# Transposing x1 on VectorE in 32x32 blocks instead of on TensorE, with the token sums taken from DRAM

## The reference

```python
x = x + _layernorm(attn(_layernorm(x)))       # attn: qkv, softmax(q k.T / 16) v, Wo, bo
x = x + _layernorm(ffn(_layernorm(x)))        # ffn: (silu(xt @ W_gate.T) * (xt @ W_up.T)) @ W_down.T, F = 2752
```

## Time and profile before

| | us |
|---|---|
| median of 3 runs | 1672.58 (1672.29 to 1673.23) |
| profiled execution | 1671.54 |
| its span in the trace | 1669.4 |
| granted TensorE clock, share of full | 0.999 |
| TensorE busy | 1651.3 (99% of the span) |
| VectorE busy | 1112.2 (67%) |
| ScalarE busy | 637.5 (38%) |
| GpSimd busy | 481.7 (29%) |
| DMA, mean over the span | 190 GB/s |

### The profile page before, as it was taken

The page is one execution under the profiler, slowest core; times in us unless marked ns, Lnnn a source line. Parts: engine busy times, 40 slices in busy tenths (PEclk is TensorE's granted clock), DMA queues, the critical chain, the costliest instruction groups (busy, mean ns, idle before and its releaser), DMA issues.

```text
span 1669.4 us, 20939 instructions
## 1 busy us (share of the span) xinstructions
PE 1651.3 (99%) x7672; PEld 1372.9 (82%) x7672; DVE 1112.2 (67%) x1625; ACT 637.5 (38%) x1149; POOL 481.7 (29%) x409
## 2 busy tenths in 40 slices
PE   7999999999999999999999999999999999999998
PEld 6888888888888888888888888888888888888887
DVE  7875677777866666666557777855655555654676
ACT  3323344445533332333246544322323333344551
POOL 3230554554345445454111102411211111200003
PEclk9999999999999999999999999999999999999999
DMA  7542564567464546464578766844444554487772
GB/s 293 202 176 78 196 219 154 176 214 254 168 221 145 170 146 191 158 216 159 171 251 320 232 205 191 261 142 139 139 142 142 160 163 147 140 284 249 226 257 101
DMA packets 161716, 317.13 MB, mean 190 GB/s; under 512 B 13008, under 2 KB 41808, under 8 KB 158672
## 3 DMA queue, kind: packets, MB, share of 16 engines
q1 hardware_dynamic: 161616, 315.82, 56.7%
HBM read 212.21 MB, written 103.56 MB: 189 GB/s over the span
## 4 chain that ended last, share of the span: by engine, by line
PE 93%; DVE 4%; DMA 1%; issue 1%; ACT 0%; POOL 0%; SPq 0%; DVEq 0%; POOLq 0%; ACTq 0%
PE ps L343 28%; PE ps L345 28%; PE ps L344 28%; PE ps L1952 4%; PE ps L1848 3%; PE ps L1953 2%; PE ps L1897 1%; PE ps L1898 1%; DMA w_raw<-hsp_dram 1%; DVE y_all L1768 1%; DVE norm_x_stats L1301 0%; DVE xn_t L1320 0%; DMA x_tile<-x 0%; DVE slots L1320 0%; DVE y_all L1824 0%
## 5 line engine op out<-in xcount | busy, mean ns | idle before, releaser
L1320 DVE TENSOR_TENSOR slots<-w_raw,slots 128x512 fp32r<-128x512 f32 x500 | 406.9, 835 | 267.4 <-ACT slots L1125 267.2
L1125 ACT CAST slots<-w_raw 128x512 fp32r<-128x512 f32 x504 | 302.1, 621 | 471.4 <-PE ps L345 461.1
L343 PE MATMUL ps<-xc,slots 128*128 128x512 f32 x1208 | 470.9, 390 | 0.3 <-issue 0.3
L345 PE MATMUL ps<-xc,slots 128*128 128x512 f32 x1208 | 470.1, 389 | 0.0
L344 PE MATMUL ps<-xc,slots 128*128 128x512 f32 x1208 | 470.0, 389 | 0.0
L343 PEld LDWEIGHTS ps<-xc,slots 128*128 128x128 f32 x1208 | 226.7, 188 | 47.6 <-issue 0.7
L345 PEld LDWEIGHTS ps<-xc,slots 128*128 128x128 f32 x1208 | 226.7, 188 | 47.1
L344 PEld LDWEIGHTS ps<-xc,slots 128*128 128x128 f32 x1208 | 226.8, 188 | 46.9
L343 PE MATMUL ps<-slots 128*128 128x512 f32 x572 | 222.6, 389 | 0.4 <-DVE slots L1320 0.4
L345 PE MATMUL ps<-slots 128*128 128x512 f32 x572 | 222.5, 389 | 0.0
L344 PE MATMUL ps<-slots 128*128 128x512 f32 x572 | 222.5, 389 | 0.0
(11 more groups left out here) (189 smaller groups left out, 2385.5 us busy)
## 6 DMA issues: line engine op xcount, KB each, us to landing
w_raw<-hsp_dram SPq DMA_DIRECT2D x154, 256.0 KB, 4.0
hsp_dram<-hs SPq DMA_DIRECT2D x20, 1792.0 KB, 8.3
w_raw<-wffn SPq DMA_DIRECT2D x134, 256.0 KB, 3.7
w_raw<-wffn SPq DMA_DIRECT2D x58, 512.0 KB, 6.2
w_raw<-wdt_dram SPq DMA_DIRECT2D x88, 256.0 KB, 3.7
wgt_dram<-tt SPq DMA_DIRECT2D x21, 1024.0 KB, 8.3
w_raw<-wgt_dram SPq DMA_DIRECT2D x84, 256.0 KB, 2.9
xc_raw<-xq_dram SPq DMA_DIRECT2D x9, 1024.0 KB, 6.7
```

Source lines behind the costliest of these rows:

```text
L343: pe.matmul(dst, stat(HIGH), mov(HIGH), start=first, stop=False, skip_group_check=reread)
L345: return pe.matmul(dst, stat(LOW), mov(HIGH), start=False, stop=last, skip_group_check=reread)
L1125: act.copy(operand(n, HIGH), source(n)).then_inc(w_high, 1)
L1320: return dve.tensor_tensor(dst, src, high.bitcast(F32), ALU.subtract)
```

## The change

VectorE transposes x1n in one instruction per tile, in 32x32 blocks, into x_cols, a buffer for four tiles (a block); nothing is transposed on TensorE for these tiles, and ScalarE's copies of them are gone. Since a block transposition leaves the 128 tokens of a tile in four groups of 32, the columns in xq_dram stand in "block order": column 128 a + 32 u + j is token 128 u + 32 a + j of the block (u the tile of the block, a the group of 32). SyncE stores a whole block at once in eight transfers of 256 KB from 32 partitions each (store_cols, in tiles 6, 10 and 14). The order within the last block is as it was. The token sums need both blocks in the same order, so they take all four parts from DRAM (load_first, 4 x 256 KB) into first_a1 and first_a2, work in place, and are done in tiles 11 to 14 (SUMS). The sums of weights move to tiles 9 and 10 (WGT = 8). load_res and store_out of blocks 0 to 2 read and write DRAM in column order (column_rows).

```diff
+SQ = 32
+WGT = KP + 1 - EARLY
+SUMS = 2 * TPB + 3
...
-    xt_tile = [at("xt_even", 188, [KC, P]), at("xt_odd", 148, [KC, P])]
-    xp_tile = at("xp_tile", 176, [2, KH, P])
-    s_tile = at("s_tile", 180, [4, KH, P])
+    x_cols = at("x_cols", 176, [KC, P // SQ, TPB, SQ])
+    first_a1 = at("first_a1", 148, [2, KH, P])
+    first_a2 = at("first_a2", 200, [2, KH, P])
...
+            def store_cols(b):
+                sp.wait_ge(cols_ready, TPB * b + TPB)
+                if b > 0:
+                    sp.wait_ge(xq_stored, 128 * b)
+                for g in range(2):
+                    for a in range(P // SQ):
+                        sp.dma_start(xq_dram[b // 2, b % 2, g, :, :, cols(a)].rearrange(
+                                         "(b j) k n -> j k b n", j=SQ),
+                                     x_cols[a * SQ:(a + 1) * SQ, KH * g:KH * g + KH, :, :, :].rearrange(
+                                         "j k b u i -> j k b (u i)")).then_inc(xq_stored, 16)
...
-            def load_partner(i):
-                sp.wait_ge(xs_done, 4 * i)
-                sp.wait_ge(xq_stored, 32 * (i + 1))
-                for g in range(2):
-                    sp.dma_start(xp_tile[:, g, :, :], xq_dram[0, 0, g, :, :, cols(i)]).then_inc(xp_loaded, 16)
+            def load_first(i):
+                sp.wait_ge(xq_stored, 256)
+                if i > 0:
+                    sp.wait_ge(xs_stored, 64 * i)
+                for block, tile in enumerate((first_a1, first_a2)):
+                    for g in range(2):
+                        sp.dma_start(tile[:, g, :, :], xq_dram[0, block, g, :, :, cols(i)]).then_inc(xp_loaded, 16)
...
+                if SUMS <= t < SUMS + TPB:
+                    load_first(t - SUMS)
                 if t == TILES - 1:
...
+                if t >= 6 and t % TPB == 2:
+                    store_cols(t // TPB - 1)
+                if SUMS <= t < SUMS + TPB:
+                    store_first_sums(t - SUMS)
                 store_x1(t - 2)
...
+            def column_rows(dram, block, i):
+                rows = dram[block * BLOCK:(block + 1) * BLOCK, :]
+                if block == BLOCKS - 1:
+                    return rows[i * P:(i + 1) * P, :]
+                return rows.rearrange("(u a j) c -> a u j c", u=TPB, j=SQ)[i]
...
             def load_res(P_, T, i, place):
-                sp.dma_start(res[:, place, :], x1_dram[row_block(2 * P_ + T, i), :]).then_inc(res_loaded[place], 16)
+                sp.dma_start(res[:, place, :], column_rows(x1_dram, 2 * P_ + T, i)).then_inc(res_loaded[place], 16)
...
+                pool.wait_ge(xp_loaded, 64 * i + 64)
+                pool.tensor_tensor(a22, a21, a22, ALU.add).then_inc(xs_done, 1)
...
                 if t == TILES - 1:
                     act.wait_ge(xs_stored, 64 * TPB)
-                    act.wait_ge(xq_stored, 32 * (LNT - 1))
+                    act.wait_ge(xq_stored, 32 * LNT)
...
+            def x1_blocks(u):
+                dve.wait_ge(x1n_done, u + 1)
+                if u >= TPB and u % TPB == 0:
+                    dve.wait_ge(xq_stored, 32 * u)
+                dve.transpose(x_cols[:, :, :, u % TPB, :].rearrange("p k b i -> p (k b) i"),
+                              x1n[:, u % 2, :].rearrange("p (m i) -> p m i", i=SQ)).then_inc(cols_ready, 1)
...
                     a_moments(t - 2)
+                if 3 <= t < last:
+                    x1_blocks(t - 3)
                 o_out(t - 1)
...
-                if t >= 4:
-                    transpose_x1n(t - 4, 0)
...
-                    if t >= 4 and g == 2:
-                        transpose_x1n(t - 4, 1)
```

More of the change, by code:

```diff
@@ L530, in store_rest_sum, with store_late @@
                 sp.dma_start(wrt_dram[:, :], w_raw[:, Q12, :]).then_inc(wgt_stored, 16)
-            def store_xq(u, g, tile):
-                sp.wait_ge(xq_evicted, 2 * u + g + 1)
-                if g == 0 and u > 0:
-                    sp.wait_ge(xq_stored, 32 * u)
-                b = u // TPB
-                sp.dma_start(xq_dram[b // 2, b % 2, g, :, :, cols(u % TPB)], tile).then_inc(xq_stored, 16)
+            def store_cols(b):
[8 more added lines that the diff above has]
+                                         "j k b u i -> j k b (u i)")).then_inc(xq_stored, 16)
+            def store_late(i, g, tile):
+                sp.wait_ge(xq_evicted, 2 * i + g + 1)
+                if g == 0:
+                    sp.wait_ge(xq_stored, 32 * (LNT + i))
+                sp.dma_start(xq_dram[1, 1, g, :, :, cols(i)], tile).then_inc(xq_stored, 16)
             def load_xc(P_, slot, block, g):
@@ L574, in _ @@
                     store_wdt(k)
[L575 removed]
+                if t == WGT:
                     load_rest()
                     load_pair(1, pair_buffer(0))
[L578 removed]
+                if t == WGT + 1:
                     store_sums(1)
                     load_pair(0)
[L581 to L589 removed]
                 if t == TILES - 1:
@@ L601, in _ @@
                     load_residual(t)
-                if t == KP + 3:
+                if t == WGT + 2:
                     store_sums(0)
@@ L680, in _ @@
                     for g in range(2):
-                        store_xq(LNT + i, g, res[:, 1, cols(g, BLOCK)].rearrange("p (k t) -> p k t", k=KH))
+                        store_late(i, g, res[:, 1, cols(g, BLOCK)].rearrange("p (k t) -> p k t", k=KH))
                 i = late_tile(p, LATE_LOAD)
@@ L1956, in weigh @@
                     last.then_inc(pv_ready, 1)
-            def transpose_x1n(u, g):
-                if g == 0:
-                    pe.wait_ge(x1n_done, u + 1)
-                else:
-                    pe.wait_ge(xq_evicted, 2 * u + 1)
-                transposes(7, KH * g, x1n[:, u % 2, :], KH).then_inc(xq_ready, 1)
             def attend(t):
```

77 lines of the change are left out of this document (23 added, 54 removed).

## The result

The changed kernel takes 1759.74 us (median of 6 runs, 1757.8 to 1761.04) against 1672.65 before; the ratio is 1.0521, 95% interval 1.0508 to 1.0535. It is 87 us slower where 34 were forecast, and lies outside the range. The span of the profiled execution is 1759.3 us against 1669.4, 89.9 more. Two much slower executions further on, 1837.64 us of rows16 and 5914.59 of early_out_plain, are not in the ratios.

What follows compares the result with a forecast made beforehand. TensorE, busy 99% of the span, was taken as the bound. Attention terms -5.4 + 8.4 + 3.8 + 2.6 = +9.4 and feed-forward +25 gave +34.4, 1707 us forecast, range 1677 to 1728.

Steps and rivals of the forecast that it cites:

- TensorE's saving: Tiles 4 to 14: without the transposes of x1n each falls from 16.84 to 16.35 us, -5.4 us together.
- VectorE's transposition: Each of twelve, between norm_a_moments and o_sum, takes 1.1 us, fits VectorE's idle gap and costs nothing.
- The loop of tiles 12 to 14: Sums, normalisation, x1 add, store and next loads take about 17.6 us against TensorE's 16.35: +3.8 us (1.2 to 6).
- Which transfers would go slowly and at what rate: Feed-forward part: 24 load_res and store_out transfers with outermost count 4 use four DMA engines, 99 GB/s, 5.3 us each.
- the start of the second pass: Eight stores and four loads on four engines, operand loads among them, outlast the operand buffers: +15 us (5 to 30).
- the end: The last four stores in groups overlap the kernel's end and cost nothing.
- Each group of four res loads: At about 925 and 1502 us: the operand load behind lands 11.6 us later, +5 each (0 to 11), together +10.
- Tile 15: ScalarE waits for column and sum stores before splitting A11, so o_half comes at 18.1 us: +2.6 (0 to 10).
- Tile 11's stall: Token sums wait for the block's return from DRAM, so VectorE normalises late and TensorE waits: +8.4 us (5.2 to 15.8).
- Sixteen engines: Rival: all sixteen DMA engines serve the 24 feed-forward transfers; +9.4, 1682 us (1675 to 1690); chance 0.18.
- Hidden stalls: Rival: the stalls are hidden and only TensorE's saving is left; 1667 us, faster; chance 0.08.
- VectorE as the bound: Rival: transposition takes 1.7 us or more and VectorE bounds tiles 4 to 14; +5.4 more, 1712 us; chance 0.06.

Runs made afterwards that it cites:

- rows16: Kernel before, with load_res and store_out of blocks 0 to 2 in 16 groups of 8 rows, 32 rows apart: 1674.22 us.
- early_out_plain: plain_rows with sums a tile later, two buffer pairs for their loads, reordered tile 15, and last o_half ahead of ScalarE's wait for the sums' stores: 1671.34 us.
- rows4: Kernel before, with load_res and store_out of blocks 0 to 2 in 4 groups of 32 rows, 128 rows apart: 1740.01 us.
- plain_rows: Changed kernel, but load_res and store_out of blocks 0 to 2 take 128 rows in a row again: 1689.85 us.
- rows4_loads: rows4 with only the twelve load_res in 4 groups, the twelve store_out as before the change: 1708.28 us.
- a11_first: plain_rows with A11 loaded ahead of block 2's column stores and split before the weight operands, ScalarE's wait for the sums' stores behind the tile: 1682.94 us.
- split_rows: Changed kernel, row order correct, each of the 24 load_res and store_out transfers cut into four of 32 rows and 32 partitions: 1692.19 us.
- rows8: Kernel before, with load_res and store_out of blocks 0 to 2 in 8 groups of 16 rows, 64 rows apart: 1695.76 us.

## Why the prediction was wrong

**Right.** TensorE's saving: 16.35 us for a tile, measured 16.32 to 16.38 in tiles 4 to 11. That the first group of transposes is worth nothing: tile 9 keeps its 0.2 us of idle. VectorE's transposition: 1.1 us forecast, 1.19 measured, with 1.03 of gap left. The loop of tiles 12 to 14: 17.6 forecast, 17.9 and 18.0 measured. Which transfers would go slowly and at what rate: 99 GB/s forecast, 98 measured, with 4.1 packets of them under way at a time; rows4 and plain_rows show the form alone to be the cause.

**What failed.** The largest miss is at the start of the second pass, where the wait was the wrong one: operands were to be late, and a store was. Three other terms had the right wait and too small a size, the end was put at nothing and so was the lower clock. All six missed on the same side.

1. *Each group of four res loads, 5 us forecast, 17.5 and 16.5 measured (rows4_loads: 16.7 and 15.3).* The operand behind them was to land at 948.5, which in the shifted time of the changed kernel is 967.9; it landed 4.5 later, at 972.4. That was an error of working, and not of the price: the operand of before came at 936.95, and four loads of 5.3 us in place of 1.3 are 16.1 more and not 11.6. From 936.95 that makes 953.0, which is 972.4 in shifted time. TensorE's reserve I had as 9.5 us from where ScalarE begins to wait; ScalarE began at 953.84 and TensorE stood from 961.35, 7.5 after it. When the operand has come, the first conversion by ScalarE and VectorE comes before the first matmul, which cost 2.1 us (972.47 to 974.53) that the reserve hid before. And TensorE starts at the lower clock. Together that is 13.2 us of wait and 4.3 beside it.

2. *The start of the second pass, +15 forecast, +31.5 measured.* I reckoned with operands behind the transfers. What comes last is the store itself: ScalarE's copy of m1 writes where y_all was and waits for the fourth store (line 1210), 26.15 us where the row of before had 3.22. I named the row and took no price from it. Up to the fourth store four stores and two loads are issued, 6 x 5.3 = 32 us on four engines from 1039.33 on, with operands among them, so it lands after 1071 at the earliest, and ScalarE wants it at 1055.5 (1058.72 less 3.22): a wait of some 16 us or more could be worked out from rows 13 and 14. rows4_loads shows it: with the stores as they were 5.5 us are left of 32.2. TensorE stands twice, 17.2 and 11.3 us, and the rest is 3.0 us, the lower clock and smaller waits.

3. *Tile 15, +2.6 forecast, +9.1 with the third round of the loop (of which 1.3 was forecast).* I worked out when A11 lands by rates alone. Block 2's eight stores held SyncE for 8.48 us and the sums' for 4.02, so A11 was issued 13.6 us after the first of them, and it took 7.8 to land, not 2.6 + 2.0, behind all that stood in the queue. a11_first takes that away and the 6.6 us with it. And tile 15's stall is paid again after it, since TensorE ran the next stretch (424 to 428) at a granted clock of 0.50: 14.1 us for work of 11.5 (a11_first).

4. *Tile 11's stall, +8.4 forecast, VectorE 11.9 late.* The loads were to have landed 18.1 us into tile 11 and GpSimd could start at 22.0. The column stores ran at 222 GB/s, not 283: 9.4 us for 2.10 MB in place of 7.4, which is 2.0 of these 3.9. I had priced slow stores only in the high end (+7.4) and taken the rate of 128 partitions for the sum. The Trainium skill, "SBUF — State Buffer", section on the DMA port swizzle, has 189 GB/s measured for partitions 0 to 31. The runs have more than that (222 here, and 235 in split_rows with operands between), but its direction was right. The other 1.9 us lie between the issue of the loads and GpSimd's start, 10.1 us, and aren't separated further.

5. *The end, nothing forecast, +5.0 measured.* The last stores in groups were to overlap the end. rows4 has the same +5.0 there and rows4_loads none, so it is the stores'. The stores of the last block stand in the queue behind them: SyncE issues the sixth of all stores of that stage 3.6 us after the fifth (1741.38 and 1745.01), where it was 0.7 before.

**What no term held: the lower clock.** After each of the long waits TensorE does its first 2.8 to 4.6 us of work at a granted clock of 0.50. The five waits are 66.1 us (10.39, 13.18, 17.23, 11.26 and 14.03); the stages in which they lie are 77.4 us longer (11.95 over 16.35 for tile 12, 17.5, 31.5 and 16.5). In all TensorE is busy for 24.4 us of the trace at 0.50, 18.9 of them behind these five waits. Work at half the clock takes twice as long (a group of four transposes 1.12 us at 349.78, where it takes 0.60), so by estimate 9.5 of the 11.3 us between are the lower clock, and the rest small waits.

**The rivals.** Sixteen engines: out, by the row with share 0.26. Hidden stalls: out. VectorE as the bound: out, by the 1.19 us of the transposition. The range was too narrow because I set the high end by one term at its end, with the others at their middle, while three of them shared one cause (loads and stores on four engines hold up everything behind them in the queue) and missed on the same side.

The Trainium skill, "DMA: Bandwidth & Descriptors", section "Why a DMA increments its semaphore by 16 and not by 1", gives the number of engines as the largest up to 16 that divides the slowest dimension of both sides. The trace agrees: 4.1, 8.1 and 16.3 packets of the loads are under way at a time in rows4, rows8 and rows16. The time of the transfers doesn't follow from it alone, 26.0, 21.1 and 10.9 us, because a packet takes 159, 300 and 246 ns.

## What to carry to other kernels

An index change that costs nothing on the engines can change the form of every transfer that meets the new order: look at the outermost count of each, and at who waits for the transfer itself, not only for what is queued behind it. Twice the engines need not halve the time: 8 groups gained 5 us of 26 on 4. Where a queue has to swallow a block at once, work out the wait of the last reader from the issue times as well as from the bytes, and give it a tile of cover and a second buffer before taking work off the busiest engine. A stall of TensorE costs more than its length here, 1.5 to 4.3 us more for 10 to 17 us, so a sum of stalls has to carry that for each piece.

## What was not expected of the hardware

- Four loads of 512 KB in rows of 4 KB, 512 packets: 9.0 us with 128 rows in a row, 26.0 in 4 strided groups, 21.1 in 8 and 10.9 in 16. The number of packets under way at a time is the count of groups, and a packet takes 159 ns in a row and in 4 groups, 300 in 8 and 246 in 16. The cause of the slower packets is open.
- Transfers from or to 32 partitions run at 222 GB/s with runs of 512 bytes and at 235 with runs of 4 KB and operands between them; with 128 partitions the two kinds of runs gave 283 and 409.
- One VectorE instruction that transposes 128x1024 fp32 in 32x32 blocks takes 1.19 us, a little less than a tensor_tensor of that size (1.22).
- SyncE takes longer to issue behind such transfers: the four res loads take 5.50 us to issue where they took 2.13, and in rows16 2.71. Whether a full queue is the reason wasn't tested.
